# Layer 0 attention: square sums of queries and keys in high and low parts, and a different order of mixing and sums

## The chip, the cores and the metric

One NeuronCore of one Trainium2 chip runs a whole four-layer network in one kernel. The metric is the device time of one execution in microseconds. Before the change the median of three runs is 1687.96 us (1687.13 to 1690.74).

## The reference, cut to what matters

The change lies in the first stage, the attention of layer 0. It has 1024 tokens (two sequences of 512), 256 features and 8 heads of 128. Queries and keys are brought to unit length, which needs the sum of squares over the 128 features of a head, for each token; then comes an attention in blocks of 64 with the block before.

```python
def _l2norm(t):
    return t / jnp.maximum(jnp.linalg.norm(t, axis=-1, keepdims=True), 1e-12)
q = (x @ Wq.T).reshape(b, n, H, DH).transpose(0, 2, 1, 3)
...
q = _l2norm(q) * q_scale
k = _l2norm(k) * k_scale
...
sim = jnp.einsum('bhnid,bhnjd->bhnij', qb * SCALE, kw)
sim = jnp.where(mask, sim, jnp.finfo(sim.dtype).min)
attn = jax.nn.softmax(sim, axis=-1)
o = jnp.einsum('bhnij,bhnjd->bhnid', attn, vw).reshape(b, H, n, DH)
```

Everything after it (the gate, the output product, the other half of layer 0 and three more layers) is left as it is.

## The kernel before, in words

All tensors lie with features on the 128 partitions and tokens along the free axis. The 1024 tokens are two chunks (c = 0, 1) of 512, which is one PSUM bank of float32, or eight tiles of 128. The eight banks are shared out by hand: banks 4 and 5 hold the projected queries of a head, 6 and 7 its keys; the pair 0 and 1 takes the scores; `SUMS = (2, 3, 0, 1)` says that the query sums go to banks 2 and 3 and the key sums to 0 and 1, after the scores have been read from there; `MIX = (2, 0)` says that the mixed values of the head before go to bank 2 (first half of the tokens) and bank 0 (second half); `TURN = (2, 3)` takes the transposed probabilities.

Each engine has its own instruction list, written out by hand, with semaphores between them. The loop over heads h on TensorE (L861 and after) does, in this order: `scores(h)`; `project(1, h + 1)`, the keys of the next head; the square sums of the next head's queries and then of its keys (`square_sums`, L856: a product of a matrix of ones with the squares, float32); the wait on the clamped query sums, then `mix_values(h - 1, 0)`; the wait on the clamped key sums, then `mix_values(h - 1, 1)`; `turn_probs(h, 0)`; `project(0, h + 2)`; `turn_probs(h, 1)`. The mixing waits because it writes into the banks from which VectorE reads the sums. Head 0 has no head before it, so its mixing is empty, but its two waits stand.

The projections (L837) already run as passes over high and low parts: an operand is copied to the type fp32r (the high part), the difference to the original is the low part, and each product is made of three passes of fp32r operands instead of one float32 product.

ScalarE per head: the high part of the weights (L962), four exponentials with sums (L985), the squares of the next keys (L971), four more exponentials, the inverse root of the query sums as a logarithm and an exponential (L979, L980), a copy of mixed values (L990), the root of the key sums, another copy, the copy of the first turned half (L1036), and the squares of the queries of head h + 2.

VectorE per head: `read_scores` for both halves (L1083 adds the mask, L1086 the maximum, L1087 its negative, which frees ScalarE's exponentials), `clamp` of the query sums (L1070, two instructions), `weigh(h, 0)` (L1093, L1094, L1095), `clamp` of the key sums, `normalise` of the queries (L1076), `weigh(h, 1)`, `normalise` of the keys, and the copy of the second turned half (L1116).

GpSimd makes the low part of the next weights once a head (L783) and nothing else in the loop. SyncE fetches the next head's weights.

Of the kernel before, what the change touches and what calls it, by code (L numbers as in the profile page):

```python
# [7 lines left out]
F32 = mybir.dt.float32  # L8
F32R = mybir.dt.float32r
I32 = mybir.dt.int32  # L10
ACT = mybir.ActivationFunctionType
ALU = mybir.AluOpType
AX = mybir.AxisListType

P = 128
# [3 lines left out]
CH = 512  # L19
NCH = T // CH  # L20
# [83 lines left out]
def over(ap, n, axis=1):  # L104

    a = ap.unsqueeze(axis)
    shape = list(a.shape)
    shape[axis] = n
    return a.to_broadcast(shape)

def chunk(c):
    return slice(c * CH, (c + 1) * CH)

def tile(t):
    return slice(t * P, (t + 1) * P)
# [592 lines left out]
def l0_attention(k, norm, mods):  # L710
# [8 lines left out]
    SCORES, SUMS, MIX, TURN = (0, 1), (2, 3, 0, 1), (2, 0), (2, 3)  # L719
# [2 lines left out]
             "q_clamped", "k_clamped", "q_root", "k_root", "q_normed", "k_normed", "scores_ready", "scores_read",  # L722
             "best_ready", "probs_exp", "probs_ready", "turned", "pt_first_copied", "pt_second_copied", "o_ready",
             "o_copied", "y_ready", "y_done", "h_hi_ready", "h_split", "wv_hi_ready", "wv_split", "w_hi_ready",
             "w_split", "v_moved")
    s = {n: k.sem("l0_" + n) for n in names}
    w_in = [k.sem(f"l0_w_in{n}") for n in range(2)]
    x_in = [k.sem(f"x_in{n}") for n in range(NCH)]
    with ExitStack() as ctx:
        def sb(n, shape, dt=F32):  # L730
            return ctx.enter_context(nc.sbuf_tensor("l0_" + n, shape, dt))
        wv = sb("wv", [P, DB, H * P])
        wv_hi, wv_lo = (sb("wv_" + n, [P, DB, H * P], F32R) for n in ("hi", "lo"))
# [11 lines left out]
        sq = norm.sq[:].rearrange("p b (c q) -> p (b c) q", q=CH)  # L745
# [5 lines left out]
        o_own = sb("o", [P, H - 3, T])  # L751
        o = [o_own[:, h] for h in range(H - 3)] + [wv[:, 0], wv[:, 1], norm.rs[:]]
        side = ("q", "k")
        first = FirstModulation(k, mods, v)

        with nc.Block() as block:
            @block.sync
# [19 lines left out]
            @block.gpsimd  # L777
            def _(pool):
                step = k.pool_chain

                def low_parts(h):
                    pool.wait_ge(s["w_hi_ready"], h + 1)
                    pool.tensor_tensor(w_lo[:, h % 2], w[:, h % 2], w_hi[:, h % 2].bitcast(F32), ALU.subtract  # L783
                                       ).then_inc(s["w_split"], 1)

                constants(k, pool)
                step.link(pool, pool.memset(qk[:, :, 0:W], 0.0))
                step.link(pool, pool.memset(mask[:, TT - 1], 0.0))
                for rows, cols, sign in ((EVEN, EVEN, 1), (EVEN, ODD, -1), (ODD, EVEN, -1), (ODD, ODD, 1)):
                    part = mask[rows, TT - 1, cols]  # L790
                    step.link(pool, pool.affine_select(out=part, in_=part, compare_op=ALU.is_ge, fill=NEG, base=0,
                                                       pattern=[[-sign, W]], channel_multiplier=sign))
                step.link(pool, pool.tensor_copy(mask[:, 0:TT - 1], over(mask[:, TT - 1], TT - 1)))
                step.link(pool, pool.memset(mask[EVEN, 0, ODD], NEG))
                pool.sem_inc(s["mask_ready"], 1)
                low_parts(0)
                pool.wait_ge(s["wv_hi_ready"], 1)
                pool.tensor_tensor(wv_lo[:], wv[:], wv_hi[:].bitcast(F32), ALU.subtract).then_inc(s["wv_split"], 1)
                low_parts(1)
                pool.wait_ge(s["w_split"], 2)  # L800
                step.link(pool, pool.memset(v_before[ODD, 0, :], 0.0))
                for t in range(TT):
                    pool.wait_ge(s["v_copied"], 2 * t + 2)
                    step.link(pool, pool.tensor_copy(v_before[EVEN, t, :], v[EVEN, t, :]))
                    if t + 1 < TT:
                        step.link(pool, pool.tensor_copy(v_before[ODD, t + 1, :], v[ODD, t, :]))
                pool.sem_inc(s["v_moved"], 1)
                for h in range(2, H):
                    low_parts(h)

            @block.tensor
            def _(pe):
# [5 lines left out]
                for t in range(TT):  # L818
                    if t % (TT // NCH) == 0:
                        norm.wait(pe, t // (TT // NCH))  # L820
                    for b in range(DB):
                        last = pe.matmul(k.bank[:, 2, t * H:(t + 1) * H], k.h[:, b, tile(t)], wg[:, b, :],
                                         start=(b == 0), stop=(b == DB - 1))
# [28 lines left out]

                def square_sums(n, h, banks):
                    for c in range(NCH):
                        pe.wait_ge(s[side[n] + "_squared"], 2 * h + c + 1)
                        pe.matmul(k.bank[:, banks[c], :], k.ones[:], sq[:, 2 * n + c, :], start=True, stop=True  # L856
                                  ).then_inc(s[side[n] + "_summed"], 1)

                def scores(h):

# [54 lines left out]
                for h in range(H):  # L915
                    scores(h)
                    if h + 1 < H:
                        project(1, h + 1)
                        if h:
                            pe.wait_ge(s["pt_first_copied"], h)  # L920
                            pe.wait_ge(s["pt_second_copied"], h)
                        square_sums(0, h + 1, SUMS[0:2])
                        pe.wait_ge(s["scores_read"], 2 * h + 2)
                        square_sums(1, h + 1, SUMS[2:4])
                    for c in range(NCH):
                        if h + 1 < H:
                            pe.wait_ge(s[side[c] + "_clamped"], 2 * h + 4)
                        elif c:
                            pe.wait_ge(s["scores_read"], 2 * h + 2)
                        else:  # L930
                            pe.wait_ge(s["pt_second_copied"], h)
                        if h:
                            mix_values(h - 1, c, MIX[c])
                    if h == H - 1:
                        project_out(range(H - 2), 0)
                    if h:
                        pe.wait_ge(s["o_copied"], 2 * h - 1)
                    turn_probs(h, 0)
                    if h + 2 < H:
                        project(0, h + 2)  # L940
                    turn_probs(h, 1)
# [13 lines left out]
            def _(act):  # L955
# [13 lines left out]
                def square(n, h, c):  # L969
                    act.wait_ge(s[side[n] + "_ready"], 2 * h + c + 1)  # L970
                    act.activation(sq[:, 2 * n + c, :], k.bank[:, 4 + 2 * n + c, :], ACT.Square  # L971
                                   ).then_inc(s[side[n] + "_squared"], 1)

                def root(n, h):

# [18 lines left out]
                for c in range(NCH):  # L994
                    norm.wait(act, c)
                    act.activation(h_hi[:, :, chunk(c)], k.h[:, :, chunk(c)], ACT.Identity
                                   ).then_inc(s["h_hi_ready"], 1)
                act.wait_ge(s["v_w_in"], 48)
                act.activation(wv_hi[:], wv[:], ACT.Identity).then_inc(s["wv_hi_ready"], 1)
                act.wait_ge(s["gate_one"], 1)  # L1000
                act.activation(gates[:], gates[:], ACT.Exp, scale=-1.0).then_inc(s["gate_exp"], 1)
                for c in range(NCH):
                    square(0, 0, c)
# [41 lines left out]
            def _(dve):  # L1045
# [21 lines left out]
                def clamp(n, h, banks):  # L1067
                    for c in range(NCH):
                        dve.wait_ge(s[side[n] + "_summed"], 2 * h + c + 1)
                        dve.tensor_scalar(rn[:, 2 * n + c, :], k.bank[:, banks[c], :], 1.0e-24, None, ALU.max  # L1070
                                          ).then_inc(s[side[n] + "_clamped"], 1)
# [30 lines left out]
                for h in range(H):  # L1102
                    for part in range(2):
                        read_scores(h, part)
                    if h + 1 < H:
                        clamp(0, h + 1, SUMS[0:2])
                    weigh(h, 0)
                    if h + 1 < H:
                        clamp(1, h + 1, SUMS[2:4])
                    if h + 1 < H:  # L1110
                        normalise(0, h + 1)
                    weigh(h, 1)
                    if h + 1 < H:
                        normalise(1, h + 1)
                    dve.wait_ge(s["turned"], 2 * h + 2)
                    dve.tensor_copy(pt[:, 4:8, :].rearrange("p t q -> p (t q)"), k.bank[:, TURN[1], :]  # L1116
                                    ).then_inc(s["pt_second_copied"], 1)
                for j in range(4):
                    m, c = j // 2, j % 2
                    dve.wait_ge(s["y_ready"], j + 1)  # L1120
                    last = dve.scalar_tensor_tensor(k.x[:, m, chunk(c)], k.bank[:, 4 + j, :],
                                                    k.mod[:, 0, GATE_A + m:GATE_A + m + 1], k.x[:, m, chunk(c)],
                                                    ALU.mult, ALU.add)
# [2636 lines left out]
```

## Time and profile before

| | us |
|---|---|
| median of three runs | 1687.96 |
| the profiled execution | 1686.74 |
| its span, first to last instruction | 1685.0 |
| layer 0 attention, up to the start of head 0's scores | 62.6 |
| from the scores of head 0 to those of head 1 | 16.2 |
| from the scores of one head to those of the next, between heads 1 and 6, each | 15.6 |
| from the scores of head 6 to those of head 7 | 14.4 |

The stage's loop over eight heads thus takes some 108 us up to the last head's scores, 6.4% of the span. PE is the matrix engine TensorE (PEld its weight loads), DVE VectorE, ACT ScalarE, POOL GpSimd.
### The profile page before, as it was taken

The page shows a single profiled execution, that of the slowest core. Times are in us where ns is not written, and L with a number is a line of the kernel's source. Part 1 is how long each engine was busy: PE and PEld are TensorE (multiplying, and loading weights), DVE is VectorE, ACT ScalarE, POOL GpSimd, SP SyncE. Part 2 cuts the span into 40 slices and gives each one's busy share as a digit, 9 for nine tenths or more (in the row PEclk, how much of TensorE's full clock was granted, in tenths as well). Part 3 has the DMA queues.
Part 4 walks back from the last instruction along what each step waited for, and adds up shares of the span by engine and source line. Part 5 has one row for each costly group of instructions (what it writes and reads, how often), then busy time and mean ns, then how long its engine had stood idle before and what let it go on. Part 6 is the DMA issues. An engine that isn't in the chain of part 4 may idle for free. (4 is left out here: it accounts for less than half of the span.)

```text
span 1685.0 us, 26919 instructions
## 1 busy us (share of the span) xinstructions
PE 1526.2 (91%) x8961; PEld 1230.1 (73%) x8962; DVE 995.4 (59%) x2349; ACT 812.7 (48%) x1782; POOL 368.9 (22%) x402
## 2 busy tenths in 40 slices
PE   8999999998729999676979998989999999999997
PEld 7777567776629998564627776867888898889665
DVE  4477272346655654344384345567777777777676
ACT  4677142343325555222755353346555566555443
POOL 3300000213076666573002121230000000000000
PEclk8999986999859999788989999999999999999999
DMA  4000040124705666431001025320000000000100
GB/s 138 14 14 1 1 160 10 38 77 111 313 25 179 187 187 184 154 104 56 1 0 38 20 70 139 93 74 20 20 19 0 19 19 19 0 19 0 50 0 25
DMA packets 56171, 109.33 MB, mean 65 GB/s; under 512 B 9937, under 2 KB 37457, under 8 KB 54458
## 3 DMA queue, kind: packets, MB, share of 16 engines
q1 hardware_dynamic: 45874, 82.10, 15.2%
q0 software_dynamic: 9168, 25.05, 5.3%
q8 instruction: 49, 0.80, 0.2%
q10 hardware_dynamic: 1040, 1.05, 0.2%
q14 instruction: 40, 0.33, 0.1%
HBM read 89.39 MB, written 18.78 MB: 64 GB/s over the span
## 5 line engine op out<-in xcount | busy, mean ns | idle before, releaser
L1886 POOL DMA_INDIRECT h_modulated<-l1f_rows,ln_rstd x127 | 119.8, 943 | 61.7 <-PE bank L1953 55.6
L3061 ACT ACTIVATE l_mem<-bank 128x129 f32<-128x129 f32 x240 | 66.4, 278 | 115.0 <-PE bank L2887 115.0
L2777 POOL COPY l_sg<-l_keys 128x512 f32<-128x512 f32 x32 | 24.2, 755 | 376.0 <-DVE l_keys L3174 376.0
L1973 PE MATMUL bank<-l1f_up,l1f_wt 128*128 128x192 f32 x508 | 104.8, 329 | 0.0
L2887 PE MATMUL bank<-l_dr,l_nkt 128*128 128x129 f32 x480 | 100.0, 293 | 1.3 <-DVE l_dr L3219 0.7
L2899 PE MATMUL bank<-l_mem,l_sg 128*128 128x129 f32 x480 | 95.4, 289 | 1.9 <-ACT l_mem L3061 0.5
L2800 PE MATMUL bank<-h_modulated,l_wo 128*128 128x128 f32 x512 | 89.3, 275 | 0.6 <-DVE h_modulated L3158 0.6
L3219 DVE SCALAR_TENSOR_TENSOR l_dr<-bank,l_inv,l_v 128x128 f32<-128x128 f32 x240 | 84.2, 351 | 8.5
L1973 PEld LDWEIGHTS bank<-l1f_up,l1f_wt 128*128 128x128 f32 x508 | 80.6, 192 | 0.1
L2887 PEld LDWEIGHTS bank<-l_dr,l_nkt 128*128 128x128 f32 x480 | 71.3, 189 | 12.3 <-DVE l_dr L3219 11.1
L2899 PEld LDWEIGHTS bank<-l_mem,l_sg 128*128 128x128 f32 x480 | 71.7, 190 | 10.4 <-ACT l_mem L3061 3.8
L2017 PE MATMUL bank<-l1f_wt,ln_square 128*128 128x128 f32 x256 | 51.0, 344 | 28.8 <-DMA ln_square<-l1f_y_rows,l1f_back_at 22.0
L1987 PE MATMUL bank<-l1f_down,ln_rstd 96*128 96x256 f32 x254 | 75.9, 380 | 0.0
L2800 PEld LDWEIGHTS bank<-h_modulated,l_wo 128*128 128x128 f32 x512 | 73.0, 192 | 0.7 <-DVE h_modulated L3158 0.7
L2222 DVE COPY l1f_wt<-bank 128x256 f32<-128x256 f32 x127 | 53.9, 424 | 30.4 <-PE bank L1953 30.4
L2017 PEld LDWEIGHTS bank<-l1f_wt,ln_square 128*128 128x128 f32 x256 | 42.3, 239 | 38.5 <-DMA ln_square<-l1f_y_rows,l1f_back_at 31.8
L1893 POOL DMA_INDIRECT ln_square<-l1f_y_rows,l1f_back_at x64 | 62.5, 977 | 30.8 <-DMA l1f_y_rows<-h_modulated 11.7
L3216 DVE RECIPROCAL l_inv<-bank 128x1 f32<-128x1 f32 x240 | 39.1, 163 | 48.8 <-PE bank L2899 47.8
L2069 ACT ACTIVATE l1f_wt<-bank 128x96 f32<-128x96 f32 x127 | 31.8, 251 | 73.8 <-PE bank L1973 73.8
L2229 DVE TENSOR_TENSOR l1f_wt<-l1f_wt,bank 128x96 f32<-128x96 f32 x127 | 32.3, 254 | 57.3 <-ACT l1f_wt L2069 33.8
L3029 ACT ACTIVATE l_e<-bank 128x512 f32<-128x512 f32 x64 | 38.3, 598 | 42.5 <-PE bank L2834 42.3
L2834 PE MATMUL bank<-l_h_hi,l_w_hi 128*128 128x512 f32 x128 | 53.1, 414 | 5.3 <-DVE l_w_lo L3135 5.3
(630 smaller groups left out, 4314.7 us busy)
## 6 DMA issues: line engine op xcount, KB each, us to landing
l1f_y_rows<-h_modulated SPq DMA_DIRECT2D x127, 128.0 KB, 1.9
l1f_up<-in_l1f_up SPq DMA_DIRECT2D x8, 1536.0 KB
l_w<-in_l_w SPq DMA_DIRECT2D x9, 768.0 KB, 4.4
l1f_down<-in_l1f_down SPq DMA_DIRECT2D x4, 1536.0 KB, 22.1
wmod<-in_wmod SPq DMA_DIRECT2D x3, 1536.0 KB, 11.5
l2e_w<-in_l2f_win SPq DMA_DIRECT2D x14, 256.0 KB, 2.8
l_w<-in_l_wqk SPq DMA_DIRECT2D x8, 256.0 KB, 2.9
l0m_w<-in_l0f_win SPq DMA_DIRECT2D x8, 256.0 KB, 2.7
```

Of the source, the lines that this page charges most:

```text
L1886: pool.indirect_dma_start(xg[:, i % GETS], None, table, bass.IndirectOffsetOnAxis(ap=listing[:, ORDER[i]:ORDER[i] + 1], axis=0)).then_inc( ...
L1893: pool.indirect_dma_start(back[:, g % BACK], None, y_rows, bass.IndirectOffsetOnAxis(ap=back_at[:, g:g + 1], axis=0)).then_inc(back_in[g % ...
L1973: last = pe.matmul(k.bank[:, UP + i % 2, 0:2 * F], xt[:, i % 2, b], of_owner(up, i)[:, :, b, :], start=(b == 0), stop=(b == DB - 1))
L1987: pe.matmul(k.bank[:, Y + i % 2, 0:D], at[:, i % 2], of_owner(experts.down, i), start=True, stop=True).then_inc(s["y_ready"], 1)
L2017: last = pe.matmul(k.bank[:, 2 * (t % 2) + m, 0:P], back[:, g % BACK, tile(m)], weigh[:, g % WEIGHS], start=(j == 0), stop=(j == TOP - 1))
L2222: dve.tensor_copy(xt[:, i % 2].rearrange("p b q -> p (b q)"), k.bank[:, XT + i % 2, 0:D]).then_inc(s["xt_copied"], 1)
L2800: last = pe.matmul(k.bank[:, Y, m * P:(m + 1) * P], wo[:, j, tile(m)], att_by_row[:, :, j, :], start=(j == 0), stop=(j == H - 1))
L2834: last = pe.matmul(k.bank[:, 4 + n, :], wq[:, b, tile(2 * a + 1 - n // 2)], hq[:, b, chunk(n % 2)], start=(q == 0), stop=(q == len(parts) ...
L2887: pe.matmul(k.bank[:, MEM + a, 0:W1], nkt[:, a, n // 2, n % 2, :], dr[:, a, n, 0:W1], start=False, stop=False, skip_group_check=True).then ...
L2899: pe.matmul(k.bank[:, READ + a, 0:W1], sg[:, a, n // 2, at:at + 2, :], mem[:, a, n % 2, 0:W1], start=True, stop=True).then_inc(s["read_rea ...
L3061: act.activation(mem[:, a, (n + 1) % 2, 0:W1], k.bank[:, MEM + a, 0:W1], ACT.Identity).then_inc(s["mem_copied"], 1)
L3219: dve.scalar_tensor_tensor(dr[:, a, n, 0:P], k.bank[:, READ + a, 0:P], inv[:, a, n % 2:n % 2 + 1], v[:, n // 2, a, n % 2, :], ALU.mult, AL ...
```

## The change

For head 1 and after (keys) and head 2 and after (queries), the sum of squares is no longer one float32 product for each chunk. ScalarE writes a second, fp32r copy of the squares (`sq_hi`) after each square; the difference to the squares (`sq_lo`) is made by GpSimd for queries and by VectorE for keys; TensorE then multiplies a fp32r matrix of ones with both parts and adds them up in the same bank. The two new tiles lie where the values' weight parts `wv_hi` and `wv_lo` were. In the loop on TensorE, the sums of the next keys move from ahead of the first half of the mixing to behind it.

```diff
+        ones_r = sb("ones_r", [P, P], F32R)
+        sq_hi, sq_lo = (m[:].rearrange("p b (c q) -> p (b c) q", q=CH) for m in (wv_hi, wv_lo))
+        SPLIT_FROM = (2, 1)
+        def split_squares(eng, n, h):
+            for c in range(NCH):
+                eng.wait_ge(s[side[n] + "_sq_hi"], NCH * (h - SPLIT_FROM[n]) + c + 1)
+                eng.tensor_tensor(sq_lo[:, 2 * n + c], sq[:, 2 * n + c], sq_hi[:, 2 * n + c].bitcast(F32), ALU.subtract
+                                  ).then_inc(s[side[n] + "_sq_split"], 1)
...
                 for h in range(2, H):
                     low_parts(h)
+                    split_squares(pool, 0, h)
...
                 def square_sums(n, h, banks):
                     for c in range(NCH):
-                        pe.wait_ge(s[side[n] + "_squared"], 2 * h + c + 1)
-                        pe.matmul(k.bank[:, banks[c], :], k.ones[:], sq[:, 2 * n + c, :], start=True, stop=True
-                                  ).then_inc(s[side[n] + "_summed"], 1)
+                        if h < SPLIT_FROM[n]:
+                            pe.wait_ge(s[side[n] + "_squared"], 2 * h + c + 1)
+                            last = pe.matmul(k.bank[:, banks[c], :], k.ones[:], sq[:, 2 * n + c, :], start=True,
+                                             stop=True)
+                        else:
+                            pe.wait_ge(s["ones_ready"], 1)
+                            pe.wait_ge(s[side[n] + "_sq_split"], NCH * (h - SPLIT_FROM[n]) + c + 1)
+                            pe.matmul(k.bank[:, banks[c], :], ones_r[:], sq_hi[:, 2 * n + c], start=True, stop=False)
+                            last = pe.matmul(k.bank[:, banks[c], :], ones_r[:], sq_lo[:, 2 * n + c], start=False,
+                                             stop=True)
+                        last.then_inc(s[side[n] + "_summed"], 1)
...
                         square_sums(0, h + 1, SUMS[0:2])
-                        pe.wait_ge(s["scores_read"], 2 * h + 2)
-                        square_sums(1, h + 1, SUMS[2:4])
                     for c in range(NCH):
                         if h + 1 < H:
+                            if c:
+                                pe.wait_ge(s["scores_read"], 2 * h + 2)
+                                square_sums(1, h + 1, SUMS[2:4])
                             pe.wait_ge(s[side[c] + "_clamped"], 2 * h + 4)
...
                     act.activation(sq[:, 2 * n + c, :], k.bank[:, 4 + 2 * n + c, :], ACT.Square
                                    ).then_inc(s[side[n] + "_squared"], 1)
+                    if h >= SPLIT_FROM[n]:
+                        act.wait_ge(s[side[n] + "_squared"], 2 * h + c + 1)
+                        act.activation(sq_hi[:, 2 * n + c], sq[:, 2 * n + c, :], ACT.Identity
+                                       ).then_inc(s[side[n] + "_sq_hi"], 1)
...
+                act.activation(ones_r[:], k.ones[:], ACT.Identity).then_inc(s["ones_ready"], 1)
                 act.wait_ge(s["v_w_in"], 48)
...
                     weigh(h, 0)
                     if h + 1 < H:
+                        split_squares(dve, 1, h + 1)
                         clamp(1, h + 1, SUMS[2:4])
```

## Rows read from the trace of the kernel before

**Rows 1.** The page: span, and TensorE's busy time, share and instructions.
```profile
span 1685.0 us, 26919 instructions
PE 1526.2 (91%) x8961; PEld 1230.1 (73%) x8962; DVE 995.4 (59%) x2349; ACT 812.7 (48%) x1782; POOL 368.9 (22%) x402
```

**Rows 2.** Busy time by stretches: start:end, length, engines' busy us, granted clock, DMA.
```profile
100.00:120.00 20.00, 20.00 (x144) 15.27 (x142) 14.87 (x29) 15.34 (x39) 1.27 (x1) 1.00 0.05 14
...
71.00:74.30 3.30, 1.15 (x7) 0.89 (x7) 3.23 (x8) 3.17 (x4) 0.00 (x0) 1.00 0.00 0
74.40:77.70 3.30, 3.30 (x9) 2.61 (x8) 1.60 (x3) 1.13 (x3) 0.00 (x0) 0.50 0.03 5
```

**Rows 3.** Timeline of TensorE, heads 2 and 3: start us, length us, instruction, count.
```profile
102.67 0.33 PE L881 MATMUL bank<-l_pt,l_v_before 128*128 128x64 f32 x2
...
106.19 0.61 PE L888 MATMUL bank<-ident,l_sc 128*128 128x128 f32 x4
...
113.42 0.61 PE L837 MATMUL bank<-l_h_hi,l_w_hi 128*128 128x512 f32 x2
113.88 0.62 PE L837 MATMUL bank<-l_h_lo,l_w_hi 128*128 128x512 f32 x2
...
114.79 3.60 PE L856 MATMUL bank<-ln_square,ones 128*128 128x512 f32 x8
118.22 0.33 PE L881 MATMUL bank<-l_pt,l_v_before 128*128 128x64 f32 x2
```

**Rows 4.** Timeline of VectorE in head 3: start us, length us, idle before it and releaser.
```profile
115.85 0.69 DVE L1070 TENSOR_SCALAR l_rn<-bank 128x512 f32<-128x512 f32 x1 [1.61 <-PE bank L856]
116.71 0.69 DVE L1070 TENSOR_SCALAR l_rn<-bank 128x512 f32<-128x512 f32 x1 [0.17 <-PE bank L856]
117.32 0.17 DVE L1093 RECIPROCAL l_st<-l_st 128x4 f32<-128x4 f32 x1
...
118.33 1.28 DVE L1070 TENSOR_SCALAR l_rn<-bank 128x512 f32<-128x512 f32 x2
119.61 1.41 DVE L1076 SCALAR_TENSOR_TENSOR l_qk<-bank,l_scales,l_rn 128x512 f32<-128x512 f32 x2
```

**Rows 5.** Groups by line and shape, 0 to 220 us: busy us, mean ns, idle before.
```profile
L1050 DVE TENSOR_TENSOR l_h_lo<-h_modulated,l_h_hi 128x1024 fp32r<-128x1024 f32 x2 | 2.4, 1221 | 0.6 <-ACT l_h_hi L996 0.6
L962 ACT ACTIVATE l_w_hi<-l_w 128x512 fp32r<-128x512 f32 x8 | 5.0, 621 | 0.0
L783 POOL TENSOR_TENSOR l_w_lo<-l_w,l_w_hi 128x512 fp32r<-128x512 f32 x8 | 10.2, 1273 | 91.3 <-ACT l_w_hi L962 91.3
```

**Rows 6.** Timeline of ScalarE in head 3: squares of keys, then the query root.
```profile
114.31 1.28 ACT L971 ACTIVATE ln_square<-bank 128x512 f32<-128x512 f32 x2
...
117.43 1.06 ACT L979 ACTIVATE l_rn<-l_rn 128x1024 f32<-128x1024 f32 x1 [0.31 <-DVE l_rn L1070]
```

**Rows 7.** Timeline of VectorE and GpSimd, columns as in rows 4.
```profile
22.98 4.38 DVE L193 TENSOR_SCALAR mod_tmp<-mod_tmp 128x2 f32<-128x2 f32 x1
28.19 0.17 DVE L193 TENSOR_SCALAR mod_tmp<-mod_tmp 128x2 f32<-128x2 f32 x1
...
22.78 4.56 POOL L798 TENSOR_TENSOR l_wv_lo<-l_wv,l_wv_hi 128x2048 fp32r<-128x2048 f32 x1 [8.46 <-ACT l_wv_hi L999]
...
110.78 1.27 POOL L783 TENSOR_TENSOR l_w_lo<-l_w,l_w_hi 128x512 fp32r<-128x512 f32 x1 [14.28 <-ACT l_w_hi L962]
...
112.55 0.17 DVE L1087 TENSOR_SCALAR l_st<-l_st 128x4 f32<-128x4 f32 x1
```

**Rows 8.** Timeline of heads 0 and 6: TensorE's waits, and VectorE ahead of one.
```profile
70.98 1.28 DVE L1070 TENSOR_SCALAR l_rn<-bank 128x512 f32<-128x512 f32 x2
...
72.36 0.63 PE L888 MATMUL bank<-ident,l_sc 128*128 128x128 f32 x4 [1.32 <-DVE l_rn L1070]
73.82 0.75 PE L837 MATMUL bank<-l_h_hi,l_w_hi 128*128 128x512 f32 x2 [0.83 <-DVE l_qk L1076]
...
170.99 2.05 PE L869 MATMUL bank<-l_qk 128*64 128x64 f32 x48 [1.54 <-DVE l_qk L1076]
```

More of the change, by code:

```diff
@@ L724, in l0_attention @@
              "o_copied", "y_ready", "y_done", "h_hi_ready", "h_split", "wv_hi_ready", "wv_split", "w_hi_ready",
-             "w_split", "v_moved")
+             "w_split", "v_moved", "ones_ready", "q_sq_hi", "k_sq_hi", "q_sq_split", "k_sq_split")
     s = {n: k.sem("l0_" + n) for n in names}
```

## The prediction

> **What bounds the kernel now.** I read the page first: TensorE is busy for 91% of a span of 1685.0 us, half as much again as VectorE with 59% [rows 1]. That is an average, so I went to the stage that the change touches. In a stretch in the middle of the head loop TensorE is busy 20.00 of 20.00 us at full clock, VectorE 14.87 and ScalarE 15.34 [rows 2]. The timeline of TensorE shows why: in the steady heads one group follows the other with no idle time, and each head takes 15.6 us. So TensorE bounds heads 1 to 5, and less work for it there is worth its time, but only if nothing it waits for gets later. The same timeline says how much is to be had. The eight records of square sums take from 114.79 to 118.22, which is 3.43 us for four float32 products, 0.86 each. Two fp32r matmuls of the same width take from 113.42 to 113.88, 0.46, so 0.23 each [rows 3]. Next the chain around the sums: VectorE's clamps wait for TensorE and start 1.06 us after their sum starts (114.79 to 115.85), 0.20 after its last column is issued, and the second ends at 117.40 [rows 3, 4]. They are over 0.8 us before TensorE wants to overwrite bank 2 at 118.22. That margin exists only because the key sums, 1.71 us, stand between. It is the cover that this change moves away.
>
> **What is removed.** Of 32 chunk sums, 7 heads of keys and 6 of queries with two chunks each, 26, go from 0.86 to 0.46 us: 0.40 each, 10.4 us of TensorE's time in all, 1.6 us in a head where both change [rows 3].
>
> **What is added on TensorE: two waits.** Let T be the start of the query sums; everything ahead of it in a head stays as it is. Before: sums to T+3.43, then two halves of mixing. From 102.67 to 106.19 these take 3.52, 1.76 each, so they end at T+6.95 [rows 3]. After:
> - Query sums end at T+0.92. The first chunk is ready at T+0.46+0.20; the clamps are a pair of 1.28 [rows 4] and end at T+1.94. A wait of TensorE on VectorE costs 0.10 more (clamp ends at 72.26, transpose starts at 72.36) [rows 8]. The first half of the mixing waits for both clamps: it starts at T+2.04, an idle time of 1.1 us that was none before, and ends at T+3.80.
> - The key sums need `sq_lo`. VectorE makes it behind `weigh`, which takes 1.01 (117.32 to 118.33) [rows 4], so from T+2.95. A difference of twice the columns takes 1.22 us [rows 5]; half is 0.61, and I take 0.66. Both are there at T+4.27: just in time for the second chunk, 0.1 late at most.
> - The first key sum ends at T+4.26, clamps run from T+4.46 to T+5.74, mixing starts at T+5.84, again 1.1 us idle, and ends at T+7.60.
> That is 0.65 us later than before. With the differences 0.1 late it is 0.75; I take 0.7. Seen as a sum: 1.6 saved, 2.3 of new idle time. Queued behind the waits are the transposes, the projection and the next scores, so the whole of it counts.
>
> **What is added on ScalarE.** Four copies to fp32r a head. The nearest row is the copy of weights of the same shape, 0.62 us [rows 5]; with the square's own completion waited for and the usual overlap of 0.1 it adds some 0.57. Two stand between the two sets of exponentials, ahead of the query root. That root starts at 117.43, T+2.64, after 0.31 us idle [rows 6], so it moves to T+3.5. Root 2.15 and normalising 1.41 [rows 4] then end near T+7.1. The projection that overwrites these banks is due at T+7.6 plus the transposes' 0.4, T+8.0. So the copies alone are hidden, with 0.9 us left. The two copies for queries fall where ScalarE waits for scores; they delay the high part of the weights by 1.15 us, and its user is most of a head away.
>
> **What is added on GpSimd.** Two differences a head. The shape is that of the weights' low part, 1.27 us each [rows 5]; GpSimd is idle 14.28 us a head [rows 7], so the 2.5 us fit. They are needed only at the next T. What they may disturb is VectorE. A VectorE instruction on two values a partition took 4.38 us instead of 0.17: it started at 22.98, while GpSimd's 4.56 us difference ran from 22.78 to 27.34, and ended just behind it [rows 7]. The Trainium skill, GPSIMD Engine Reference, section Key points, says that GpSimd shares its SBUF interfaces with VectorE and contends with instructions in a 2-port mode or with two SBUF inputs; the trace agrees with its 4.38 us, and by that rule each new difference can hold an instruction of VectorE. In the loop the one at risk is L1087 at 112.55, of the same kind as the one held. Now GpSimd is done at 112.05; 1.15 us later and behind the new differences it works until 113.2 to 113.8, so L1087, and with it the exponentials, may come 0.6 to 1.2 us late. That takes the normalised queries from T+7.1 to between T+7.7 and T+8.3, against T+8.0 due. Bounds 0 and 0.3 us a head, I take 0.1.
>
> **Sum.** Heads 1 to 5: 0.7+0.1, 0.8 each, 4.0 us. Head 0: its query sums stay float32 and there is no mixing to hide behind. The key clamps stood right behind `weigh`, 70.98 to 72.26 [rows 8]. Now the two differences stand there until 72.3; the second key sum starts at 72.4, ends at 72.86, and its clamp runs from 73.06 to 73.75. The transposes and all behind come 1.5 us later. Head 6: it has no projection of queries behind it, and TensorE already waits 1.54 us for the normalised keys [rows 8]. The later mixing goes into that wait. The keys' root is held by ScalarE, whose added time of 1.15 meets the later mixing it waits for anyway: the key clamps end at T+5.74 instead of T+4.82, but the key root could not begin before T+5.8 even now, so 0.2 is left (bounds 0 and 1.2). The small copy of the ones, 128 columns, lies ahead of a stretch in which the values' low part is ready at 27.34 and wanted 6 us later: nothing. In all 1.5+4.0+0.2, 5.7 us. The profiled execution took 1686.74 us, 1.74 around its span, and becomes 1692.4. It lies 1.2 under the median of 1687.96, so the forecast of a median is 1693.7. From the bounds (0.65 to 1.05 a head, head 6 up to 1.2, head 0 by 0.2 either way) this case alone reaches from 1692.5 to 1696.0, and by the spread of the runs shown, 3.6 us, from 1691 to 1697.
>
> **The rivals.**
> - The clock falls in the heads. After TensorE stood idle for 1.32 and 0.83 us close together in head 0 the granted clock was 0.50 in the next stretch of 3.3 us [rows 2, 8]; that costs half of it, 1.65 us. For it: two idle times of 1.1 us in every head, and longer ones in head 0. Against: after a single 1.54 at 170.99 [rows 8] nothing fell, and the two new ones are 2.7 us apart with dense work between. If it decided in heads 1 to 6 it would cost 9.9 more: 1703.6. Chance 0.09.
> - GpSimd holds VectorE more than once a head. If L1087 is held by 1.2 and then one of VectorE's own differences or `weigh` as well, the normalised queries pass T+8.0 by 1.2 us. That decides in six heads: 7.2 more, 1700.9. The rule named above would speak for it; the rows show one such hold, none in this loop. Chance 0.12.
> - Only one of the two waits is paid. If the clamps of the keys were ready when the mixing wants their bank, a head would save 0.4 instead of losing 0.7: 5 times -0.4, plus 1.7 of heads 0 and 6, is -0.3, 1687.7, no change. It needs key sums that start about 1 us before the first half of mixing ends, or clamps that need not both be done. The order in the code speaks against both. What could also bring it near is latencies of the waits that are half of what I read. Chance 0.16.
> - Faster: the clamps don't hold TensorE at all and the 10.4 us of removed matrix time reach the end: 1677.6. It decides only if mixing could go ahead of the clamps in bank 2, which the wait on both clamps forbids; the new idle time could then only be paid by something that I read wrongly, such as fp32r sums that let VectorE start far sooner. Chance 0.06.
> The forecast itself holds 0.57.
>
> **How the numbers follow.** The likeliest case gives 1693.7. About 0.2% or 3.4 us is what a measurement of this kernel can tell from no change, so slower means above 1691.3 and faster below 1684.6. Slower: 0.57+0.09+0.12, less 0.03 for the lower edge of the forecast, 0.75. Same: 0.16+0.03, 0.19. Faster 0.06. The range leaves out the faster case and the fallen clock in every head, and takes in one wait paid and GpSimd's holds: 1687.0 to 1701.0.
>
> **What would show it.** In the profile after, square sums of keys and queries as fp32r pairs 0.46 us apart; TensorE idle for about 1.1 us ahead of each half of the mixing, with L1070 as releaser; scores of heads 1 to 6 spaced by 16.4 instead of 15.6, head 0 17.7 instead of 16.2, head 6 near 14.5; L1087's first half at or behind the end of a GpSimd difference; TensorE's busy time some 10 us less and the span longer all the same. The prediction is wrong if those idle times are under 0.8 us, if the granted clock falls inside heads 1 to 6, or if a wait on normalised queries stands ahead of the projection with more than 0.3 us.

## The result, and the profile after

The changed kernel takes 1699.33 us, median of seven runs (1697.08 to 1703.78), against 1691.42 of seven runs of the kernel before (1687.13 to 1692.53). The ratio is 1.0062, 95% interval 1.0044 to 1.0080: slower, by 7 to 14 us, most likely 10.5. The two medians by themselves differ by 7.9 us, which lies in the same interval. Run once more beside other kernels (e7_after_again below) the ratio was 1.0095 (1.0063 to 1.0126). The forecast was slower by 5.7 us.

The profiled execution has a span of 1697.6 us, 12.6 more than before. This table says where they arise. The stage's end is taken at the first product of the next stage (the line `l0f_wq`), all times from the timelines.

| us | before | after | difference |
|---|---|---|---|
| up to the scores of head 0 | 62.6 | 63.6 | +1.0 |
| head 0 to head 1 | 16.2 | 18.1 | +1.9 |
| head 1 to head 6, five heads | 77.8 | 81.6 | +3.8 |
| head 6 to head 7 | 14.4 | 16.7 | +2.3 |
| scores of head 7 to the stage's end | 49.2 | 50.4 | +1.2 |
| all behind the stage | 1464.8 | 1467.3 | +2.4 |

The page's head, to set beside [rows 1]:

```profile
span 1697.6 us, 26991 instructions
PE 1530.6 (90%) x8962; PEld 1238.3 (73%) x8962; DVE 1005.3 (59%) x2363; ACT 827.7 (49%) x1809; POOL 384.3 (23%) x414
```

TensorE was to be busy for 10 us less, and is for 4 more. In the stage it is busy for 151.3 us instead of 152.9: much of what it saves in columns it loses at a lower clock, as will be seen. Behind the stage, where the code is the same, it is busy for 5.0 us more, with 196.3 us of half clock there instead of 179.1. A steady head on TensorE, which answers [rows 3] (timeline: start us, length us, instruction, idle time before it and its releaser):

```profile
135.53 0.39 PE L872 MATMUL bank<-l_wv_hi,l_ones_r 128*128 128x512 f32 x1
135.75 0.39 PE L873 MATMUL bank<-l_wv_lo,l_ones_r 128*128 128x512 f32 x1
135.98 0.39 PE L872 MATMUL bank<-l_wv_hi,l_ones_r 128*128 128x512 f32 x1
136.21 0.39 PE L873 MATMUL bank<-l_wv_lo,l_ones_r 128*128 128x512 f32 x1
137.52 0.44 PE L899 MATMUL bank<-l_pt,l_v_before 128*128 128x64 f32 x2 [0.93 <-DVE l_rn L1094]
...
140.14 0.40 PE L873 MATMUL bank<-l_wv_lo,l_ones_r 128*128 128x512 f32 x1
141.43 0.43 PE L899 MATMUL bank<-l_pt,l_v_before 128*128 128x64 f32 x2 [0.89 <-DVE l_rn L1094]
...
143.62 0.71 PE L847 MATMUL bank<-l_h_hi,l_w_hi 128*128 128x512 f32 x2
```

Read it with T = 135.53: the four passes start 0.23 apart, a chunk's sum is 0.45 us instead of 0.86. Then TensorE waits for the clamps, twice, and the mixing starts at T+1.99 and T+5.90. The idle times are a little longer than the brackets say, because a matmul's recorded end lies behind the start of the next: from T+0.91, where the passes are issued, to T+1.99 is 1.1 us. The second one lies between T+4.84, 0.23 behind the last pass of the key sums at 140.14, and T+5.90, again 1.1 us. VectorE and GpSimd in the same head, for [rows 4] and [rows 7]:

```profile
133.30 0.92 DVE L1111 TENSOR_SCALAR l_st<-l_st 128x4 f32<-128x4 f32 x1
...
136.18 1.29 DVE L1094 TENSOR_SCALAR l_rn<-bank 128x512 f32<-128x512 f32 x2 [0.44 <-PE bank L873]
...
138.40 1.29 DVE L762 TENSOR_TENSOR l_wv_lo<-ln_square,l_wv_hi 128x512 fp32r<-128x512 f32 x2
140.08 1.29 DVE L1094 TENSOR_SCALAR l_rn<-bank 128x512 f32<-128x512 f32 x2 [0.40 <-PE bank L873]
141.80 1.41 DVE L1100 SCALAR_TENSOR_TENSOR l_qk<-bank,l_scales,l_rn 128x512 f32<-128x512 f32 x2 [0.43 <-ACT l_rn L1003]
...
130.31 2.64 POOL L762 TENSOR_TENSOR l_wv_lo<-ln_square,l_wv_hi 128x512 fp32r<-128x512 f32 x2 [12.44 <-ACT l_wv_hi L994]
132.90 1.29 POOL L792 TENSOR_TENSOR l_w_lo<-l_w,l_w_hi 128x512 fp32r<-128x512 f32 x1
```

The small instruction L1111 lasts 0.92 us instead of 0.17: it starts at 133.30, while GpSimd works until 134.19, and ends at 134.22. The same happens in each of heads 1 to 5, and not in heads 0 and 6. Last the clock, for [rows 2], busy time by stretches (start:end, length, busy us and count of PE, PEld, DVE, ACT, POOL, then granted clock, DMA share, GB/s):

```profile
100.00:120.00 20.00, 18.17 (x139) 15.03 (x136) 16.05 (x29) 15.94 (x41) 5.34 (x5) 1.00 0.10 26
...
73.30:79.90 6.60, 5.52 (x15) 3.70 (x14) 4.99 (x10) 3.39 (x5) 0.00 (x0) 0.50 0.00 0
...
168.80:172.10 3.30, 2.37 (x19) 1.95 (x19) 3.21 (x7) 3.27 (x12) 0.00 (x0) 1.00 0.00 0
172.20:182.30 10.10, 9.32 (x61) 8.03 (x62) 6.07 (x12) 5.22 (x7) 0.00 (x0) 0.50 0.01 2
```

In head 0 the clock was at 1.2 GHz for 6.8 us, where it was for 3.4 before. In the second half of head 6 it fell from 2.4 to 1.2 GHz and stayed there for 10.2 us, into the scores of head 7. What TensorE did before it fell was this, the first of the two idle times and the mixing behind it; the second idle time had not begun:

```profile
170.16 0.44 PE L899 MATMUL bank<-l_pt,l_v_before 128*128 128x64 f32 x2 [0.93 <-DVE l_rn L1094]
...
171.97 0.62 PE L872 MATMUL bank<-l_wv_hi,l_ones_r 128*128 128x512 f32 x1
172.39 0.63 PE L873 MATMUL bank<-l_wv_lo,l_ones_r 128*128 128x512 f32 x1
```

### The profile page after: what moved, and what is told of

Its sections match the earlier page's. It is cut to its first block and busy times, and to the rows that moved or that the text cites. A ratio compares the mean times of both kernels' runs of the same rounds, so it can differ in the third digit from the quotient of the medians.

```text
span 1697.6 us, 26991 instructions
## 1 busy us (share of the span) xinstructions
PE 1530.6 (90%) x8962; PEld 1238.3 (73%) x8962; DVE 1005.3 (59%) x2363; ACT 827.7 (49%) x1809; POOL 384.3 (23%) x414
## 3 DMA queue, kind: packets, MB, share of 16 engines
q1 hardware_dynamic: 45874, 82.10, 15.1%
## 5 line engine op out<-in xcount | busy, mean ns | idle before, releaser
L1918 POOL DMA_INDIRECT ln_square<-l1f_y_rows,l1f_back_at x64 | 62.6, 978 | 31.2 <-issue 12.5
```

The lines of the kernel that those rows point to most:

```text
L1918: pool.indirect_dma_start(back[:, g % BACK], None, y_rows, bass.IndirectOffsetOnAxis(ap=back_at[:, g:g + 1], axis=0)).then_inc(back_in[g % ...
```

## The experiments

The theory after the first comparison: the heads themselves lose what was forecast, 0.78 us each, and what stands above that in the stage comes from falls of the clock which the new idle times bring on. The rival: those falls, like the many in later stages, come wherever they come, and the heads have nothing to do with it.

All ratios below are to the kernel before, run on the same chip in the same session. The ratios of e10_fill_second and e3_split_only rest on four runs of the kernel, the others below on ten to twelve. The single profiles of the stage are compared by its length from the scores of head 0 to its end, since what is ahead of it varies by 1.5 us from profile to profile: 157.6 us before, 166.7 after.

**e1_fill: the two idle times filled.** The changed kernel, and a product of zeros in each.

```diff
                             if c:
                                 pe.wait_ge(s["scores_read"], 2 * h + 2)
                                 square_sums(1, h + 1, SUMS[2:4])
+                                k.idle_products(pe, 1, 3)
+                            else:
+                                pe.wait_ge(s["scores_read"], 2 * h + 2)
+                                k.idle_products(pe, 1, 0)
                             pe.wait_ge(s[side[c] + "_clamped"], 2 * h + 4)
```

> The changed kernel, with one product of zeros (float32, 512 columns, 0.86 us) put into each of the two new idle times of a head: into bank 0 ahead of the wait on the clamped query sums, into bank 3 ahead of the wait on the clamped key sums. They fit into 1.1 us of idle time, so by the timeline alone nothing moves: heads 1 to 5 stay at 16.3 us. Theory A (what stands above the two waits in the measured difference is clock falls brought on by the idle times): the granted clock stays at 1.00 in heads 1 to 7, head 6 goes from 16.7 to 14.5 to 15.0 us, the scores of head 7 from 3.2 to 2.1, and the time is some 3 to 5 us under the changed kernel, a ratio to before near 1.003. Rival B (the rest is where the clock happens to fall in later stages, whatever the heads do): the ratio stays at 1.006.

Measured: 1.0024 (1.0006 to 1.0043). The stage is 161.4 us long. Stretches of its profile, one for each head:

```profile
62.00:78.00 16.00, 13.62 (x92) 9.25 (x92) 11.41 (x22) 12.46 (x30) 1.40 (x2) 1.00 0.06 17
...
127.00:143.00 16.00, 15.91 (x123) 12.55 (x122) 12.92 (x23) 13.64 (x32) 3.68 (x3) 1.00 0.01 3
...
160.00:174.00 14.00, 13.52 (x112) 10.49 (x112) 11.73 (x23) 11.70 (x29) 2.07 (x2) 1.00 0.00 0
```

The clock is 1.00 in all of them, in head 0 too. Heads 1 to 5 still take 16.33 us each: the added products are 0.86 us long and fit into the idle time, so they don't lengthen a head. Head 6 takes 14.46 instead of 16.66. More work on TensorE and a shorter stage, by 5.3 us: this is what the falls cost there, and it speaks for the theory. The interval of the ratio ends where that of the changed kernel begins, so the runs bear it out, narrowly.

**e7_after_again: the changed kernel once more**, without an edit.

> The changed kernel once more, without any edit, on the chip of the two others. Theory A, clock falls brought on by the two idle times of each head: falls inside the heads are there again, not necessarily in the same heads, 10 to 25 us of half clock between the scores of head 0 and the end of the stage, and the stage ends 8 to 12 us later than before. Rival B: this profile shows heads without a fall beyond head 0, the stage ends 5 us later than before, and the rest comes from later stages. Heads without a fall take 16.3 us in both.

Measured: 1.0095 (1.0063 to 1.0126). The stage is 168.4 us long. One stretch:

```profile
139.10:149.20 10.10, 9.32 (x32) 7.71 (x32) 5.18 (x10) 6.36 (x10) 0.00 (x0) 0.50 0.01 2
```

The fall has moved from head 6 to head 4, which takes 20.55 us, 4.2 more than its neighbours; heads 1 to 3 and 5 take 16.33, head 6 14.46. In head 0 there is one of 6.8 us again, 18.79 us. Both profiles have 17.1 us of half clock between head 0's scores and the stage's end, before had 3.4. The falls come again, in another head. Together with e1 this settles the rival for the stage. The profile is of the fastest of ten runs (1696.07 us); three others took 1716 to 1719, and no profile shows where they lost it.

**e9_fill_first and e10_fill_second: one of the two filled.** As e1, with only the product ahead of the first, or only that ahead of the second half of the mixing.

> The changed kernel with the first of the two idle times of each head filled, ahead of the first half of the mixing; the second, 1.1 us, stays. If one idle time of 1.1 us in a head is enough for the clock to fall, falls inside heads 1 to 7 are there and the stage ends 7 to 11 us after before's. If it takes both, they are gone beyond head 0, and the stage ends 3.5 to 6 us later. Heads without a fall 16.3 us.

> The changed kernel with the second idle time of each head filled, ahead of the second half of the mixing; the first stays. Same two readings as for e9_fill_first: falls in heads 1 to 7 if one idle time is enough, none if it takes both. In head 0 the long idle time ahead of the key sums, 2.5 us, stays, so a fall there is expected either way.

Measured: e9 1.0041 (1.0016 to 1.0067), an interval that overlaps that of the changed kernel; its profile has a stage of 161.4 us with no fall, every head as in e1:

```profile
63.00:190.00 127.00, 117.39 (x914) 91.20 (x913) 93.69 (x173) 98.02 (x236) 22.86 (x18) 1.00 0.03 9
```

For e10 it was 1.0073 (1.0053 to 1.0093), a stage of 164.8 us with three short falls, in heads 0, 1 and 3:

```profile
72.10:75.30 3.20, 2.86 (x6) 1.85 (x7) 2.26 (x5) 1.47 (x3) 0.00 (x0) 0.50 0.00 0
89.20:92.40 3.20, 3.20 (x8) 1.92 (x8) 2.61 (x4) 3.17 (x4) 0.00 (x0) 0.50 0.00 0
123.30:126.50 3.20, 3.20 (x9) 1.94 (x9) 2.72 (x5) 3.17 (x4) 0.00 (x0) 0.50 0.00 0
```

Heads 1 and 3 take 17.65 us there, heads 2, 4 and 5 16.33. So the first idle time of 1.1 us is enough. That both are needed is refuted; that the second alone does nothing rests on one profile. The two expectations gave each kernel the same two outcomes; that the first idle time matters and the second alone doesn't was not foreseen. The starts of the falls agree with it: in head 6 of the changed kernel, head 4 of e7 and heads 1 and 3 of e10 the clock fell 4.0 to 4.3 us behind the start of the query sums, and the second idle time begins only at 4.8. With both, falls last 10.2 us in heads, with the first alone 3.4. These are single profiles; that the second one prolongs a fall is likely, not shown.

**e2_order_only: the order of the change, sums as before.**

```diff
                         square_sums(0, h + 1, SUMS[0:2])
-                        pe.wait_ge(s["scores_read"], 2 * h + 2)
-                        square_sums(1, h + 1, SUMS[2:4])
                     for c in range(NCH):
                         if h + 1 < H:
+                            if c:
+                                pe.wait_ge(s["scores_read"], 2 * h + 2)
+                                square_sums(1, h + 1, SUMS[2:4])
```

> The kernel before with the new order alone: all sums stay float32 products of 0.86 us, the key sums stand behind the first half of the mixing. If the two idle times come from the order and from nothing else, they are there in full, about 1.0 us each, and nothing is saved: heads 1 to 5 at 17.6 us instead of 15.55, head 0 about 0.4 more, head 6 about 1.3 more, 11 to 12 us slower than before without any clock fall. If the idle times came from the late low parts of the key squares, which this kernel doesn't have, heads would stay near 15.6.

Measured: 1.0041 (1.0017 to 1.0065). A steady head:

```profile
118.00 1.88 PE L856 MATMUL bank<-ln_square,ones 128*128 128x512 f32 x4
120.66 0.43 PE L881 MATMUL bank<-l_pt,l_v_before 128*128 128x64 f32 x2 [0.78 <-DVE l_rn L1071]
122.50 1.94 PE L856 MATMUL bank<-ln_square,ones 128*128 128x512 f32 x4
125.22 0.43 PE L881 MATMUL bank<-l_pt,l_v_before 128*128 128x64 f32 x2 [0.78 <-DVE l_rn L1071]
```

And the stretch of the heads up to the scores of head 7:

```profile
62.00:182.00 120.00, 107.56 (x803) 80.05 (x803) 76.32 (x147) 79.90 (x193) 7.64 (x6) 1.00 0.04 10
```

Both idle times are there without any low part, from 118.00+1.71 to 120.66, 0.95 us. Heads 1 to 5 take 17.65 us, as expected. The idle time thus belongs to the order. The clock doesn't fall in this profile, not even in head 0, which takes 15.1 us where 0.4 more than before's 16.2 was expected. So two idle times of 0.95 us in every head don't bring the falls on by their mere presence. What sets this kernel apart from the changed one (each is 0.15 us shorter, and the sums before them are float32 products) was not varied, and which of it matters stays open. The stage is 168.3 us long, 10.7 over before, but the runs differ by about 7 (3 to 11 by the interval), so the profile is at the upper edge of what the runs say.

**e3_split_only: high and low parts with the order of before.** The reverse of e2's edit on the changed kernel.

> The changed kernel with the order of before: both sums ahead of the mixing, in high and low parts. The key sums wait for VectorE's low parts, which lie behind weigh: one idle time of 2.8 us instead of two of 1.1. By the chain heads 1 to 5 take 16.9 us, 0.6 more than the changed kernel, head 0 as there, head 6 15.9, so 8 to 10 us slower than before, and more if the longer idle time makes the clock fall in every head. If the new order were the harm, this kernel would be faster than the changed one, near 15.0 a head.

Measured: 1.0143 (1.0104 to 1.0183), 24 us slower and by far the slowest. The stage is 190.9 us long. The wait, and the clock by heads:

```profile
87.43 0.47 PE L872 MATMUL bank<-l_wv_hi,l_ones_r 128*128 128x512 f32 x1 [2.63 <-DVE l_wv_lo L762]
```

```profile
79.00:100.00 21.00, 18.37 (x116) 16.15 (x117) 12.92 (x23) 13.55 (x32) 3.32 (x3) 0.76 0.04 13
101.00:123.00 22.00, 19.37 (x112) 17.03 (x109) 12.70 (x23) 13.56 (x31) 3.29 (x4) 0.69 0.04 13
124.00:145.00 21.00, 18.37 (x116) 16.16 (x115) 12.95 (x23) 13.52 (x32) 2.57 (x3) 0.76 0.04 13
146.00:162.00 16.00, 13.37 (x113) 11.43 (x109) 12.65 (x23) 13.17 (x31) 3.05 (x3) 1.00 0.00 1
```

Head 4, without a fall, takes 16.96 us, just what the chain gave. The others of heads 1 to 5 take 21.8 to 23.2. With one idle time of 2.8 us the clock falls in five of heads 0 to 6, all but 0 and 4, and a fall of 10.2 to 13.7 us costs 4.8 to 6.2. So the low parts without the new order are worse than with it: the reordering mends a part of what the splitting of the keys does. At full clock that is 0.6 of the 2.0 us a head by which this kernel (16.96) lies above e4 below (14.92), where the keys are not split; in the whole time it is 8 to 14 of 30 us by the ratios. The expectation named clock falls in every head as a possibility and didn't price it.

**e4_queries_only: high and low parts for the queries alone.** The key sums stay float32 and in their old place, where they cover the clamps.

```diff
-        SPLIT_FROM = (2, 1)
+        SPLIT_FROM = (2, H)
...
-                        split_squares(dve, 1, h + 1)
...
+                        pe.wait_ge(s["scores_read"], 2 * h + 2)
+                        square_sums(1, h + 1, SUMS[2:4])
                     for c in range(NCH):
                         if h + 1 < H:
-                            if c:
-                                pe.wait_ge(s["scores_read"], 2 * h + 2)
-                                square_sums(1, h + 1, SUMS[2:4])
```

> High and low parts for the queries alone (GpSimd makes the low part), key sums as float32 products, order of before. The cover of 1.7 us of key sums stands again, so no idle time of TensorE on the clamps. By TensorE's work a head saves 0.8 us, 14.75. But GpSimd's work now holds L1087's counterpart by some 0.75 us, and with it the exponentials: if that reaches the normalised keys or queries, heads come to 15.1, 3 us faster than before in all; if the hold costs nothing, 14.75 and 4.8 us faster. Rival: no gain at all, if the chain of exponentials, roots and normalising is as long as TensorE's work.

Measured: 0.9965 (0.9945 to 0.9985), faster than the kernel before. Heads 1 to 5 take 14.92 us, between the two values given; the stage is 153.6 us long, 4.0 shorter. GpSimd's hold is there, the counterpart of L1087 in this kernel:

```profile
110.75 0.93 DVE L1110 TENSOR_SCALAR l_st<-l_st 128x4 f32<-128x4 f32 x1
```

**e5_queries_dve: the low parts moved from GpSimd to VectorE.**

```diff
-                    split_squares(pool, 0, h)
...
                         read_scores(h, part)
+                    if 2 <= h + 1 < H:
+                        split_squares(dve, 0, h + 1, (1,))
...
                         normalise(1, h + 1)
+                    if h + 2 < H:
+                        split_squares(dve, 0, h + 2, (0,))
```

> As e4_queries_only, but VectorE makes the low parts of the query squares, one chunk ahead of the copy of the turned half, one behind the reading of the scores, both in time that it stands idle; GpSimd makes only the weights' low part, as before. If GpSimd's hold on VectorE's small instruction is what keeps e4 at 14.92 us a head above the 14.75 of TensorE's own work, this kernel comes to 14.75, one us under e4 over six heads, and the instruction that lasts 0.93 us there lasts 0.17. If the hold costs nothing and something else is late, heads stay at 14.9.

Measured: 0.9958 (0.9929 to 0.9986). Heads 2 to 5 take 14.74 us, head 1 14.78, and the stage is 152.8 us long. The small instruction is nearly back at its length:

```profile
111.18 0.21 DVE L1109 TENSOR_SCALAR l_st<-l_st 128x4 f32<-128x4 f32 x1
```

So the hold cost 0.18 us a head in e4. It is small; the ratios of e4 and e5 can't tell it.

**e6_queries_fill0: e4, and head 0's idle times filled** with two products of zeros.

```diff
                             pe.wait_ge(s[side[c] + "_clamped"], 2 * h + 4)
+                            if h == 0 and c == 0:
+                                k.idle_products(pe, 1, 3)
...
                     turn_probs(h, 0)
+                    if h == 0:
+                        k.idle_products(pe, 1, 3)
```

> As e4_queries_only, with two products of zeros of 0.86 us in the idle times of head 0, one behind the wait on the clamped query sums, one behind the first transposes. Theory: the fall of the clock in head 0, which before and e4 show, is brought on by these idle times; filled, the clock stays up and head 0 goes from 16.2 to 14.6 us, 1.6 us faster than e4. Rival: the fall comes all the same, or the products delay the transposes, and head 0 stays at 16.2.

Measured: 0.9956 (0.9929 to 0.9984). Head 0 takes 14.59 us instead of the 16.2 of before and of e4, at full clock; the stage is 152.1 us long, 1.6 under e4:

```profile
71.53 1.02 PE L95 MATMUL bank<-zeros,ident 128*128 128x512 f32 x2
72.97 0.66 PE L906 MATMUL bank<-ident,l_sc 128*128 128x128 f32 x4 [0.42 <-DVE l_rn L1097]
73.47 1.02 PE L95 MATMUL bank<-zeros,ident 128*128 128x512 f32 x2
74.47 0.70 PE L847 MATMUL bank<-l_h_hi,l_w_hi 128*128 128x512 f32 x2
```

**e8_best: e5 and e6 together.**

> e5_queries_dve and the two products of e6_queries_fill0 together: query sums in high and low parts with VectorE's low parts, key sums float32, order of before, head 0 filled. If the two gains are separate they add: head 0 14.6 us, heads 1 to 5 14.75, head 6 13.6, the stage over 6.3 us earlier than before, ratio 0.994 to 0.996. If not, the clock falls in head 0 or heads stay at 14.9.

Measured: 0.9958 (0.9939 to 0.9977). The stage is 151.1 us long, 6.5 shorter than before, with 14.60 in head 0 and 14.74 in the others: the gains add in the stage. In the whole time they can't be told from e4's. The stage's gain is 6.5 us, the runs show 3.9 to 10.3. In the profiled execution the span is even 1689.0, since the part behind the stage took 1474.5 us instead of 1464.8, with 215.6 us of half clock there against 179.1. That part is the same code in all kernels; in the twelve profiles, two of them of the changed kernel, it took 1460.9 to 1474.5.

## Why the prediction was right and wrong

It forecast slower and it is slower, within the stated range, and the steps about the heads were right to within 0.2 us wherever the clock stayed up. The size was too small: 5.7 forecast, 10.5 by the ratio. That 1699.33 lies inside the range is partly luck: its upper end of 1701.0 came from the rival of GpSimd's repeated holds, which did not happen, and the second timing, 1.0095, would be 1704.0 on the median of 1687.96 and outside it.

- Sums: 0.46 forecast, 0.45 measured for the queries and 0.55 for the first key sum (its clamps start at 140.08, 0.20 behind it). TensorE's start behind VectorE's end: 0.10 forecast, 0.05 measured (137.47 to 137.52). Mixing at T+2.04 and T+5.84 forecast, T+1.99 and T+5.90 measured. Differences of VectorE 1.29 a pair, 1.32 forecast.
- Steady heads: 0.8 more forecast, 0.78 measured, 3.8 us for five instead of 4.0.
- GpSimd's hold: L1087's counterpart 0.6 to 1.2 us late forecast, 0.75 measured. Normalised queries end at T+7.68, ahead of the T+8.0 at which they are due, so nothing waits for them; the 0.1 that I took for it is not there, and the differences and latencies make up the same sum. By e4 and e5 the hold costs 0.18 us a head where TensorE has no idle time. The Trainium skill, GPSIMD Engine Reference, section Key points, says that the two engines share SBUF interfaces and contend when VectorE's instruction is in a 2-port mode or has two SBUF inputs. The trace shows one hold in each of heads 1 to 5; in which mode the held instruction runs no run here shows.
- Head 0: 1.5 forecast at the clock of before. With its idle times filled it takes 16.1 us, 1.5 more than the 14.6 of e6, which has before's sums of head 0 and no fall either. So the step was right, and the error in this head is the clock: in both profiles of the changed kernel the fall there lasts 6.8 us instead of 3.4.
- Head 6: 0.2 more forecast. e1 has 14.46 and e7 14.46, 0.05 more than before.

The step that failed is the clock. The sum took the clock of before for all heads and held nothing for new falls; they stood only in the first rival. I argued that two idle times of 1.1 us with dense work between would not bring it on, because one of 1.54 us at 170.99 had not, and gave it 0.09, as something that decides in all heads or in none. It decides in one head now and another then: head 6 with 10.2 us of half clock in one profile, head 4 in the other, and longer falls in head 0. The prediction had named a fall inside heads 1 to 6 as a sign that it is wrong, and that sign is there. One idle time of 1.54 us without a fall was no evidence for seven heads with two each.

The term that was missing in the sum can be read from the lengths of the stage. Without any fall (e1) the changed kernel's stage is 3.8 us longer than before's (157.6 to 161.4), which has one. That one cost 1.6 (e6 against e4), so with no fall on either side the change adds 5.4, near the 5.7 of the forecast. The falls of the changed kernel, 17.1 us of half clock, cost 5.3 and 6.9 us in its two profiles against e1, 3.7 and 5.3 more than before's 1.6. So the stage got 9.1 and 10.8 us longer. The share of the clock in the full runs is an estimate from these profiles. The ratios of e1 (1.0024) and of the two timings of the changed kernel (1.0062 and 1.0095) differ by 6 and 12 us, which agrees with it in sign, for the first timing also in size; the second is nearly twice what its profile shows, and e9, whose profile has no fall either, lies between with 1.0041. Why the clock falls in one head and not in the next, and not at all in e2, stays open.

What is left of the 12.6 us between the two profiled executions is not the change's: 1.0 ahead of the stage, where a fall of the clock in the first projections lasted longer (e7 starts its heads at 62.45, earlier than before), and 2.4 behind it, within the spread of that part.

The change does save TensorE's columns. The new order helps because the low parts of the key squares come late, as e3 shows, but it leaves two waits, and together they cost more than they give. The half of it that has cover, the queries, is worth 4 us.

## What to carry to other kernels

A block of work that looks like cost can be the cover of a wait: before making it shorter or moving it, find out which chain ends under it, and by how much. Where TensorE is busy without a gap, price a new idle time twice, once for its length and once for the chance that the clock falls, per place and not all or none; a product of zeros into a free bank in the gap tells the two apart, as it did here. Low parts are cheap where their operand is ready half a head early (queries) and dear where it is ready just in time (keys).

## What the runs showed of the hardware

- With one idle time of 1.1 us in heads of 16.3 us the clock fell to 1.2 GHz in some heads and not in others of the same execution (e10: heads 1 and 3), while the kernels with this idle time filled showed no fall in the stage (e1, e9). Two idle times of 0.95 us in heads of 17.65 us showed none either (e2).
- A fall inside a head cost 1.3 us when it lasted 3.4 us (e10), and 4.2 us when it lasted 10.2 us (e7), somewhat less than half of its length; why less was not tested. In e10 TensorE was busy for all of the 3.2 us shown, so its waits don't explain it there.
- A GpSimd instruction on two tensors held a VectorE instruction of four elements a partition (L1111, from SBUF to SBUF) until it ended: 0.92 us instead of 0.17 in heads 1 to 5. Not every instruction is held: the reduction just ahead of it lasts 0.69 us beside the same GpSimd work, as it does before.

```profile
132.57 0.69 DVE L1110 TENSOR_REDUCE l_st<-l_sc 128x4 f32<-128x512 f32 x1
```
